# Cross attention and MLP on one core: on-chip tensors laid out in another order, at other start offsets within 512 bytes

## The reference

```python
def _cross_attention(q_in, kv_in, ...):          # 16 heads of 128
    qh, kh, vh = q_in @ wq + bq, kv_in @ wk + bk, kv_in @ wv + bv
    kh, vh = concat(kh, bias_k), concat(vh, bias_v)     # one learned key and value
    weights = softmax(qh @ kh.T / sqrt(128))
    return (weights @ vh) @ wo + bo
x = x + cross_attention(layer_norm(x), ctx)      # twice, with weights 1 and 2
x = x + gelu(layer_norm(x) @ w_fc1 + b_fc1) @ w_fc2 + b_fc2
```

## Time and profile before

| | us |
|---|---|
| median of three runs | 497.98 (497.58 to 499.17) |
| the profiled execution, its own time | 496.78 |
| span of its trace | 495.0 |
| TensorE busy with products | 489.1 |
| TensorE busy with weight loads | 444.5 |
| POOL, DVE, ACT busy | 413.7, 391.2, 331.0 |

### The profile page before, as it was taken

The page is one execution under the profiler, slowest core; times in us unless marked ns, Lnnn a source line. Parts: engine busy times, 40 slices in busy tenths (PEclk is TensorE's granted clock), DMA queues, the critical chain, the costliest instruction groups (busy, mean ns, idle before and its releaser), DMA issues.

```text
span 495.0 us, 11021 instructions
## 1 busy us (share of the span) xinstructions
PE 489.1 (99%) x3228; PEld 444.5 (90%) x3228; DVE 391.2 (79%) x911; ACT 331.0 (67%) x727; POOL 413.7 (84%) x387
## 2 busy tenths in 40 slices
PE   8999999999999999999999999999999999999997
PEld 6888998998998998999988989999989989999997
DVE  4889877888878878866789888788788888766896
ACT  3777767667775866666486877758666677768441
POOL 4877989989898998997597999989989898999542
PEclk9999999999999999999999999999999999999999
DMA  7435886756667676612115786676767566650001
GB/s 272 149 104 170 265 249 197 208 187 195 187 195 209 192 229 190 181 58 66 42 44 164 267 236 184 203 199 202 222 189 209 181 195 179 206 156 1 23 23 42
DMA packets 52901, 82.56 MB, mean 167 GB/s; under 512 B 5882, under 2 KB 33934, under 8 KB 52878
## 3 DMA queue, kind: packets, MB, share of 16 engines
q1 hardware_dynamic: 52878, 82.28, 54.5%
HBM read 53.42 MB, written 28.84 MB: 166 GB/s over the span
## 4 chain that ended last, share of the span: by engine, by line
PE 91%; DVE 6%; DMA 1%; POOL 1%; ACT 1%; issue 0%; DVEq 0%; POOLq 0%
PE ring L1190 68%; PE ps_ctx L1190 11%; PE acc L1190 9%; PE ring L1236 1%; DVE v_lo L1174 1%; DVE k_hi L1172 1%; DVE k_lo L1174 1%; DMA probs<-ctx_in 1%; DVE v_hi L1172 1%; DVE h_lo L971 0%; DVE pT_lo L890 0%; PE ring L1545 0%; DVE z_sb L951 0%; PE ring L1273 0%; DVE k_lo L825 0%
## 5 line engine op out<-in xcount | busy, mean ns | idle before, releaser
L905 DVE TENSOR_REDUCE row_max<-ring 128x1 f32<-128x512 f32 x112 | 76.1, 688 | 27.8 <-PE ring L1190 27.7
L634 ACT ACTIVATE probs<-ring,shift 128x512 f32<-128x512 f32 x112 | 76.4, 682 | 18.9 <-DVE shift L910 18.8
L415 POOL TENSOR_TENSOR v_lo<-v_sum,v_hi 128x512 fp32r<-128x512 f32 x64 | 82.9, 1297 | 2.7 <-ACT v_hi L584 2.7
L868 DVE STREAM_TRANSPOSE blocks<-probs 128x512 f32<-128x512 f32 x108 | 70.1, 687 | 4.9 <-POOL probs L422 4.6
L422 POOL TENSOR_SCALAR probs<-probs,inv 128x512 f32<-128x512 f32 x80 | 55.2, 696 | 20.3 <-DVE inv L918 20.2
L427 POOL TENSOR_TENSOR pT_lo<-wf_lo,pT_hi 128x1024 fp32r<-128x1024 f32 x28 | 67.0, 2412 | 0.0
L1190 PE MATMUL ring<-pT_lo,v_hi 128*128 128x256 f32 x208 | 58.4, 281 | 0.2 <-DVE pT_lo L890 0.2
L566 ACT ACTIVATE k_hi<-ring,cols 128x512 fp32r<-128x512 f32 x57 | 37.8, 688 | 31.0 <-PE ring L1190 30.8
L1190 PE MATMUL ring<-pT_hi,v_lo 128*128 128x256 f32 x208 | 58.1, 279 | 0.0
L1190 PE MATMUL ring<-pT_hi,v_hi 128*128 128x256 f32 x208 | 58.0, 279 | 0.0
L1190 PE MATMUL ring<-wv_lo,cT_hi 128*128 128x256 f32 x196 | 54.8, 279 | 0.0
(11 more groups left out here) (208 smaller groups left out, 1631.8 us busy)
## 6 DMA issues: line engine op xcount, KB each, us to landing
spill<-blocks SPq DMA_DIRECT2D x54, 512.0 KB, 2.9
wf_lo<-spill SPq DMA_DIRECT2D x112, 128.0 KB, 3.2
wf_hi<-spill SPq DMA_DIRECT2D x104, 128.0 KB, 3.2
wk_raw<-wk_in SPq DMA_DIRECT2D x17, 256.0 KB, 2.8
wq_raw<-wq_in SPq DMA_DIRECT2D x17, 256.0 KB, 3.4
wv_raw<-wv_in SPq DMA_DIRECT2D x16, 256.0 KB, 3.7
vrows<-vrows_in SPq DMA_DIRECT2D x16, 256.0 KB, 4.0
wo_raw<-wo_in SPq DMA_DIRECT2D x16, 256.0 KB, 2.7
```

The costliest lines, as they stand in the source:

```text
L415: pool.tensor_tensor(v_lo[:, 2 * m:2 * m + 2, :], v_sum[:, m % 2, :].rearrange("p (t c) -> p t c", c=PW), v_hi[:, 2 * m:2 * m + 2, :].bitc ...
L634: act.activation(probs[:, u, q, :], ring[S_BANKS[where][QTB * u + q]][:], ACT.Exp, bias=shift[:, u, q:q + 1], scale=SCALE, accum_out=row_s ...
L868: last = dve.transpose(blocks[:, u % 2, :, :, q, :].rearrange("p g c b -> p c g b"), probs[:, u, q, :].rearrange("p (c g b) -> p c g b", g ...
L905: dve.reduce_max(row_max[:, u, q:q + 1], ring[S_BANKS[where][QTB * u + q]][:], AX_X).then_inc(max_done, 1)
```

## The change

The tensors are allocated in another order, with three small fillers between them. `begin_at(offset)` adds a filler so that the next tensor starts at that offset within 512 bytes. Small tensors come first, then all large ones from offset 0, then the value weights from 64, the output weights from 128 and the transposed probabilities from 256. No instruction is added, removed or moved, and no operand's shape or type changes.

```diff
--- before.py
+++ after.py
@@ -1,3 +1,4 @@
+import math
 from contextlib import ExitStack
 
 import concourse.bass as bass
@@ -65,14 +66,27 @@
 G_LAG = 6
 WF1_PARTS = FB // PW
 WARM_UP, KEEP_WARM = 5, 2
+
+
+
+SB_FIRST, SB_GRAIN, ROW_BYTES = 16512, 32, 512
 LOAD = 16
 
 
 def build_program(nc, spill, x_in, ctx_in, wq_in, wk_in, wv_in, wo_in, vrows_in, head_rows_in,
                   dim_rows_in, out_rows_in, wf1_in, wf2_in, out):
     with ExitStack() as stack:
+        taken = []
+
         def sb(name, shape, dt=F32):
+            taken.append(-(-4 * math.prod(shape[1:]) // SB_GRAIN) * SB_GRAIN)
             return stack.enter_context(nc.sbuf_tensor(name, shape, dt))
+
+        def begin_at(offset):
+
+            gap = (offset - SB_FIRST - sum(taken)) % ROW_BYTES
+            if gap:
+                sb(f"filler{offset}", [P, gap // 4])
 
         def sem(name):
             return stack.enter_context(nc.semaphore(name))
@@ -81,18 +95,27 @@
         ring.append(stack.enter_context(nc.psum_tensor("ps_ctx", [P, 512], F32)))
         acc = [stack.enter_context(nc.psum_tensor(f"acc{i}", [P, 512], F32)) for i in range(2)]
 
-        ident = sb("ident", [P, P])
-        zeros = sb("zeros", [P, 512], F32R)
         minus_half = sb("minus_half", [P, QT])
         head_rows = sb("head_rows", [P, P])
         dim_rows = sb("dim_rows", [20, P])
         head_cols = sb("head_cols", [P, 4, LAYERS * HEADS])
-
         step_cols = sb("step_cols", [P, ALL_PAIRS + 2, 3, 2])
         cols = sb("cols", [P, 3, 2])
         dim_cols = sb("dim_cols", [P, 20])
         table_load = sb("table_load", [P, 1])
-        out_rows = sb("out_rows", [P, NORMS, D])
+        bn = sb("bn", [P, QT, 6])
+        mean_var = sb("mean_var", [P, QT, 2])
+        var_eps = sb("var_eps", [P, QT])
+        rstd = sb("rstd", [P, QT])
+        row_max = sb("row_max", [P, NU, QTB])
+        shift = sb("shift", [P, NU, QTB])
+        p_learned = sb("p_learned", [P, NU, QTB])
+        row_sum = sb("row_sum", [P, NU, QTB])
+        total = sb("total", [P, NU, QTB])
+        inv = sb("inv", [P, NU, QTB])
+        vbias = sb("vbias", [P, PW])
+        begin_at(0)
+        zeros = sb("zeros", [P, 512], F32R)
         cT_hi = sb("cT_hi", [P, DC, CT * P], F32R)
         cT_lo = sb("cT_lo", [P, DC, CT * P], F32R)
         x_sb = sb("x_sb", [P, QT, D])
@@ -101,37 +124,31 @@
         h_full = sb("h_full", [P, DC, TOK])
         h_hi = sb("h_hi", [P, DC, TOK], F32R)
         h_lo = sb("h_lo", [P, DC, TOK], F32R)
-        bn = sb("bn", [P, QT, 6])
-        mean_var = sb("mean_var", [P, QT, 2])
-        var_eps = sb("var_eps", [P, QT])
-        rstd = sb("rstd", [P, QT])
         wq_raw = sb("wq_raw", [P, DC, PW])
         wk_raw = sb("wk_raw", [P, DC, PW])
         wv_raw = sb("wv_raw", [P, DC, PW])
         wo_raw = sb("wo_raw", [P, 2, D])
         wq_hi, wq_lo = sb("wq_hi", [P, DC, PW], F32R), sb("wq_lo", [P, DC, PW], F32R)
         wk_hi, wk_lo = sb("wk_hi", [P, DC, PW], F32R), sb("wk_lo", [P, DC, PW], F32R)
-        wv_hi, wv_lo = sb("wv_hi", [P, DC, PW], F32R), sb("wv_lo", [P, DC, PW], F32R)
-        wo_hi, wo_lo = sb("wo_hi", [P, 2, D], F32R), sb("wo_lo", [P, 2, D], F32R)
         vrows = sb("vrows", [P, 2, PW])
-        vbias = sb("vbias", [P, PW])
         q_hi, q_lo = sb("q_hi", [P, 2, TOK], F32R), sb("q_lo", [P, 2, TOK], F32R)
         k_hi, k_lo = sb("k_hi", [P, 2, CT * P], F32R), sb("k_lo", [P, 2, CT * P], F32R)
         v_sum = sb("v_sum", [P, 2, 2 * PW])
         v_hi, v_lo = sb("v_hi", [P, CT, PW], F32R), sb("v_lo", [P, CT, PW], F32R)
         probs = sb("probs", [P, NU, QTB, CLEN])
-        row_max = sb("row_max", [P, NU, QTB])
-        shift = sb("shift", [P, NU, QTB])
-        p_learned = sb("p_learned", [P, NU, QTB])
-        row_sum = sb("row_sum", [P, NU, QTB])
-        total = sb("total", [P, NU, QTB])
-        inv = sb("inv", [P, NU, QTB])
         blocks = sb("blocks", [P, 2, QB, CTB, QTB, BLK])
-        pT_hi, pT_lo = sb("pT_hi", [P, 2, CTB, QLEN], F32R), sb("pT_lo", [P, 2, CTB, QLEN], F32R)
         o_hi, o_lo = sb("o_hi", [P, 2, TOK], F32R), sb("o_lo", [P, 2, TOK], F32R)
         wf_raw = sb("wf_raw", [P, 2, 512])
         wf1_hi, wf1_lo = sb("wf1_hi", [P, DC, FB], F32R), sb("wf1_lo", [P, DC, FB], F32R)
         wf2_hi, wf2_lo = sb("wf2_hi", [P, FT, D], F32R), sb("wf2_lo", [P, FT, D], F32R)
+        out_rows = sb("out_rows", [P, NORMS, D])
+        ident = sb("ident", [P, P])
+        begin_at(64)
+        wv_hi, wv_lo = sb("wv_hi", [P, DC, PW], F32R), sb("wv_lo", [P, DC, PW], F32R)
+        begin_at(128)
+        wo_hi, wo_lo = sb("wo_hi", [P, 2, D], F32R), sb("wo_lo", [P, 2, D], F32R)
+        begin_at(256)
+        pT_hi, pT_lo = sb("pT_hi", [P, 2, CTB, QLEN], F32R), sb("pT_lo", [P, 2, CTB, QLEN], F32R)
 
         wf2_spare = [w[:].bitcast(F32).rearrange("p f d -> p (f d)") for w in (wf2_hi, wf2_lo)]
```

## The result

The change makes the kernel slower: 500.75 us (median of 6 runs, 499.65 to 501.35) against 498.08 (496.76 to 499.17, 6 runs), a ratio of 1.0054 with an interval of 1.0037 to 1.0071. Forecast were 491.7, and a chance of 0.60 of faster. It went the way of rival 3 (501.8).

The account below looks back on a forecast made before the run. TensorE's product pace bounds the kernel; long products gain 0.11 us and short 0.28 per step, 0.39 together, over 17.1 steps' worth 6.7, taken as 6.3: 491.7 us. Range for 8 in 10: 485.5 to 501.0; the forecast's own 489 to 495.

Parts of the forecast that it names:

- rival 3: Short products lock at the high, slower pace, 14.18 us per step; step 28.04, kernel 501.8 us; chance 0.23.
- What bounds the kernel: Loop steps: TensorE busy for all of 27.82 us, so only the pace of its 180 products counts.
- The long products: S, K and Q blocks, all at distance 0: 1.375 us per block, 13.75 per step, a gain of 0.11.
- I trust most: First step's long run of K and Q: pace falls from 0.229 to 0.226 us per product.
- The short products: V, C and O at new distances: 1.37, 1.37 and 1.36 us for 12, 13.68 per step, a gain of 0.28.
- Rows 6: Profile rows of the MLP's short products over wf1, distance 128 before the change: 0.119 us each.
- The phase: Loop steps: long products at equal offsets leave another phase behind, a weak reason for short products near the better bound.
- The MLP: Mostly short products, moved to distance 0: taken at the same share as the rest, losing the 0.119 over wf1.
- Rival 2: Placement hardly matters, alternation of long and short products sets the paces: 497.4 us, or 496.3 to 499; chance 0.22.
- the rule beside it: TensorE has SBUF read ports of its own and never waits, so placement changes nothing: 498.0 us.
- Rival 4: Another engine, POOL, bounds a faster step and could clip single steps: 492 to 494 us; chance 0.04.
- How it turns into time: Whole kernel: 17.1 steps' worth times 0.39 us is 6.7, of which 6.3 us was taken as gain.

Follow-up runs that it names:

- `long_only`: Changed kernel with value weights, output weights and probabilities back at their old distances, long products staying at distance 0: 497.86 us, 0.999 of before.
- `phase`: TensorE alone, 24 short products at distance 192, 64, 144 or 0, entered after one product of 256 to 286 columns: settled paces 113.3 to 120.0 ns.
- the replica: TensorE alone running a step's products in their order, without waits, for 20 operand layouts: 27.81 us in the layout of before, 27.99 in the changed one.
- `all_144`: Changed kernel with value weights, output weights and transposed probabilities all at 144, long products at distance 0: 495.40 us, 0.9948 of before.
- `at_112_112_192`: Changed kernel with value weights and transposed probabilities at 112 and output weights at 192: 495.12 us, 0.9943 of before.
- `distances`: Kernel without the computation, TensorE alone running long and short products at 16 operand distances: settled long 226.7 to 234 ns, short 116.7 to 120.0.

## Why the prediction was wrong

**What bounds the kernel** held. TensorE is busy through every step, and the pace of its products is the time. That no engine, queue or wait makes the difference between the two kernels' steps was right as well.

**The long products** held, in size too: forecast a gain of 0.11 us in a step, measured 0.112. The long run fell from 0.229 to 0.2265, the step "I trust most". That the mean of the ten blocks came out at my 1.375 is in part luck. I took it for each of them, because I took the short products in front of them to be at their lower pace. These are at the higher one, and no block takes 1.375: five lock at 1.36 (both Q, two of four K, one of four S) and five stay at 1.39.

**The short products** are the step that failed. The prediction took them "near the better one" of two bounds, "V and C at 1.37 for 12", "O at 1.36", a gain of 0.28. Measured is a loss of 0.285: V at 1.41 to 1.42, C between 1.42 and 1.45, OO at 1.42. Even my worst bound, 14.18 in a step, was passed by 0.07, since C at 256 goes up to 120 ns in one block. The reason given for the side, "there is more room on this side than on the other", is no reason at all: how many products are at the high pace says nothing of where a new distance puts them. What the runs show in its place: V went from 192, which meets 113.3 ns from 10 of 16 entries, to 64, which meets it from 1; C went from 192 to 256, which is 0 again, 120 ns; O from 320, which is 64, to 128, 120 ns (118.7 behind other long products, and 118.6 to 119.3 in the kernel). All three went to a worse place. Rows 6 had 128 at 0.119 and were the only rows that bore on a new distance; rival 3 read them, and came within 1.1 us of the time. Its sizes were off in opposite directions, 0.07 us per step too little for the short products and 0.11 too much for the long ones, and no run tests the mechanism that it gave, a load held up by the moving stream. The measured time lies inside my range for 8 in 10 only because that range reached up to just under this rival.

**The phase** was half right. The prediction said of V that "the offsets alone don't decide, what ran before does too"; `long_only` shows it, and `phase` bears it out. But it then counted that in its favour ("leave another phase behind"), where `long_only` shows the opposite: with only the long ones moved, the short ones lose 0.14 us.

**The MLP** went the other way too. It was taken "at the same share as the rest" and "should lose its 0.119"; its short products, now at distance 0, went up to 0.120.

**Rival 2 and the rule beside it** fell. By the page SBUF — State Buffer of the Trainium skill (section Who interferes with whom) TensorE's reads never wait on anyone. TensorE alone on the core ran its short products at 113 to 130 ns by nothing but their operands' distance and what ran before; the replica and the two kernels agree to the ns. Whoever else is on the core is no part of it, in that the rule agrees; that placement is free does not follow.

**Rival 4** can't be judged from this change, which made no step shorter; `all_144` shows how far it goes, two steps of ten, and `at_112_112_192` has none.

**How it turns into time** was right to some 10%. The 17.1 steps' worth were counted from 20 us on. From the second step of the first loop on it is (495.0 - 66.84)/27.82 = 15.4, times 0.173 is 2.66 us, against 2.98 measured there in the traces and 2.67 between the medians.

**Open**: by what mechanism the distances differ. The replica predicts an undisturbed step to 1 ns; the table of 32 distances doesn't, since one distance can have two paces, and I have no rule from which 112, 192 and 104 come out.

## What to carry to other kernels

When a stretch is bound by one engine's back-to-back products, their spacing is a quantity of its own: sum the gaps between starts by kind, over all products, before changing anything. Don't guess what a new operand placement does; a kernel with nothing but the products, in the real order, gives the step to the ns in one run, for twenty layouts at once. What it can't give are the steps in which another engine holds TensorE up; there `all_144` lost part of its gain. Treat equal offsets as something to be measured for each shape: here they are the best for 512 columns and among the worst for 256.

## What the runs showed of the hardware

- With a weight load before every product, float32-rounded operands and the high clock, 256 columns mostly take 113.3, 116.7, 117.8, 118.7 or 120.0 ns (256/2.4 = 106.7 would be the stream), up to 130.0, and 512 columns 226.7, 229 or 233.3 (213.3). The start of the moving operand minus that of the stationary one, modulo 256 bytes, and what ran before decide. The page TensorE: Matmul & The Clock Gate of the Trainium skill (section Wait — 56ns, not 53.3ns?) gives N/2.4 + 2.5 ns, 215.7 measured for 512 columns; no settled run here is under 226.
- The patterns are deterministic: undisturbed steps repeat to 1 ns within a trace, and `all_144` and its replica, on two different chips, agree at 27.600 us.
- In the first 3 us of products in `distances` each long one took 427 ns, 512/1.2, the pace of the lower clock, whereas the granted clock of that window reads 1.00. Window, then PE, PEld, ACT, POOL, clock, DMA share, GB/s:

```profile
12.96:15.95 2.99, 2.98 (x7) 2.41 (x8) 0.00 (x0) 0.00 (x0) 1.00 0.00 0
```

  Seven products in 2.99 us are 0.427 each, and the page TensorE: Matmul & The Clock Gate of the Trainium skill (section Wait — 56ns, not 53.3ns?) gives 426.7 for that clock, which agrees. The column reads 1.00 everywhere in this trace, which holds no clock record, though the gap per long product falls to 227 ns later on. So I trust the gaps, not the column.
